# Columns for the sort by target loaded during the sort by source, and four groups folded before the bits are made, in a graph kernel on one core

## The reference, cut to what matters

```python
for l in range(3):                       # first network
    xi, xj = x[src], x[dst]
    e = relu((xj - xi) @ theta[l].T + xi @ phi[l].T)
    agg = segment_max(e, src)            # by source
    x = relu(batch_norm(agg) * gamma[l] + beta[l])
# second, third and fourth network: sums over edges by target (dst),
# with edge_type (16 kinds) and edge_weight for each edge
```

## Time and profile before

| | |
|---|---|
| median of 3 runs | 7136.56 us (7126.43 to 7139.59) |
| the profiled execution's own time | 7128.72 us |
| its span in the trace | 7127.0 us |
| DVE busy | 4064.9 us (57%) |
| POOL busy | 3651.3 us (51%) |
| PE busy | 2465.0 us (35%) |
| mean granted TensorE clock | 0.664 |

### The profile page before, as it was taken

How to read it: one execution, slowest core, us unless ns; L and a number is a source line. 1 busy time by engine, 2 the same in 40 slices (tenths; PEclk the granted TensorE clock), 3 DMA queues, 4 the chain that set the end, 5 groups by cost and what they waited for, 6 DMA issues and landing times. The chain is left out here.

```text
span 7127.0 us, 70146 instructions
## 1 busy us (share of the span) xinstructions
PE 2465.0 (35%) x10688; PEld 1392.0 (20%) x10714; DVE 4064.9 (57%) x10627; ACT 1532.5 (22%) x3929; POOL 3651.3 (51%) x3557
## 2 busy tenths in 40 slices
PE   4477000445566666980006950011001300000038
PEld 3333000322243333440003420001000300000025
DVE  8997454477757765443335444354445466666661
ACT  1165000122236652113332113320001000000011
POOL 0000577477657760017761037755774477777720
PEclk9999555755587887995558975555555755555569
DMA  0001455466545541336653336643663465655610
GB/s 3 0 0 41 156 192 197 133 204 206 187 135 188 187 166 48 153 122 205 210 196 110 153 136 209 210 140 134 208 207 110 149 190 188 190 185 187 190 63 18
DMA packets 334787, 1052.51 MB, mean 148 GB/s; under 512 B 72272, under 2 KB 107632, under 8 KB 288080
## 3 DMA queue, kind: packets, MB, share of 16 engines
q0 software_dynamic: 181456, 515.80, 24.7%
q1 hardware_dynamic: 153216, 535.47, 19.3%
HBM read 534.80 MB, written 516.19 MB: 147 GB/s over the span
## 5 line engine op out<-in xcount | busy, mean ns | idle before, releaser
L940 POOL DMA_INDIRECT rows<-typed_table,index x832 | 813.0, 977 | 1185.6 <-DVE index L964 932.8
L940 POOL DMA_INDIRECT out_of<-table,index x936 | 970.5, 1037 | 465.1 <-issue 283.9
L979 DVE SCALAR_TENSOR_TENSOR state<-state,by_target_keep,rows 128x256 f32<-128x256 f32 x1248 | 604.9, 485 | 950.1 <-ACT rows L958 544.7
L940 POOL DMA_INDIRECT rows<-table,index x728 | 730.5, 1003 | 317.9 <-issue 221.5
L2211 PE MATMUL bank<-weights,out_of 128*128 128x512 f32 x1600 | 698.8, 595 | 26.6 <-DVE weights L2259 26.6
L979 DVE SCALAR_TENSOR_TENSOR y<-y,by_source_anew,out_of 128x256 f32<-128x256 f32 x897 | 435.9, 486 | 294.9 <-DMA out_of<-table,index 196.6
L1109 PE MATMUL bank<-ident,tail 128*128 128x128 f32 x6 | 2.0, 433 | 1658.2 <-PEq L74 1658.2
L2355 POOL DMA_INDIRECT qv<-qv_table,index x416 | 495.3, 1191 | 143.7 <-issue 126.4
L958 ACT ACTIVATE rows<-rows,by_target_weight 128x256 f32<-128x256 f32 x832 | 343.1, 494 | 753.8 <-DMA rows<-typed_table,index 753.8
L2358 POOL DMA_INDIRECT k<-k_table,index x416 | 433.2, 1041 | 126.8 <-issue 126.8
L1739 PE MATMUL bank<-x,marks 128*128 128x416 f16 x1664 | 395.4, 410 | 218.0 <-ACT marks L1753 218.0
(11 more groups left out here) (438 smaller groups left out, 6513.9 us busy)
## 6 DMA issues: line engine op xcount, KB each, us to landing
states<-state SPq DMA_DIRECT2D x195, 1024.0 KB, 4.3
states<-y SPq DMA_DIRECT2D x117, 1024.0 KB, 4.5
typed_table<-staged SPq DMA_DIRECT2D x400, 256.0 KB, 2.0
wide_states<-y SPq DMA_DIRECT2D x26, 1088.0 KB, 5.6
wide_states<-state SPq DMA_DIRECT2D x26, 1088.0 KB, 5.6
out_of<-table,index POOLq DMA_INDIRECT x936, 2.9
rows<-typed_table,index POOLq DMA_INDIRECT x832, 2.9
rows<-table,index POOLq DMA_INDIRECT x728, 2.9
```

Source lines behind the costliest of these rows:

```text
L940: pool.indirect_dma_start(out=rows[h][:, u * D:(u + 1) * D], out_offset=None, in_=table, in_offset=bass.IndirectOffsetOnAxis(ap=index[h][: ...
L979: nc.vector.scalar_tensor_tensor(out=state[h][:, u * D:(u + 1) * D], in0=before, scalar=marks[:, bass.ds(g * GROUP + u, 1)], in1=rows[h][: ...
```

## The change

The four columns for the sort by target are loaded by SP during the first step of `edge_order`, after POOL has filled their tiles; the edge type goes straight to `by_target.row`, and the source shifted by 4 is put in by an OR. `TargetSort.pad` fills only `z`. In the first pass DVE waits for the remaining four loads, folds groups 0 to 3, then runs `CountTargets.ahead`, and then the one-hot tiles of the groups 0 to 3 in one run; from group 4 on each group's one-hot tiles follow its fold as before. The second and third pass are as they were.

```diff
--- before.py
+++ after.py
@@ edge_order
-def edge_order(nc, env, order):
+def edge_order(nc, env, order, target, given):
...
-        names = ("hot", "w_ready", "turned", "copied", "counted", "count_kept", "compared", "ranked", "held")
+        names = ("hot", "w_ready", "turned", "copied", "counted", "count_kept", "compared", "ranked", "held", "padded", "loaded")
...
+            columns = ((target.node, given["dst"], ROWS - 1), (target.source, given["src"], ROWS - 1), (target.row, given["edge_type_16"], 0),
+                       (target.weight, given["edge_weight"], 0.0))
+
+            @block.gpsimd
+            def _(pool):
+                for tile, _, fill in columns:
+                    pool.memset(tile[:], fill).then_inc(padded, 1)
+
+            @block.sync
+            def _(sp):
+                sp.wait_ge(padded, len(columns))
+                for tile, dram, _ in columns:
+                    sp.dma_start(tile[0:P - 1, :], dram[0:(P - 1) * STEPS].rearrange("(p t) -> p t", t=STEPS)).then_inc(loaded, 16)
+                    sp.dma_start(tile[P - 1:P, 0:TAIL], dram[(P - 1) * STEPS:E].unsqueeze(0)).then_inc(loaded, 16)
+                sp.wait_ge(loaded, 32 * len(columns))
+
@@ edge_pass
-                def fold_group(i, h, more=True):
+                def fold_group(i, h, more=True, alone=False):
...
-                    if beside:
+                    if beside and not alone:
                         beside.group(dve, g, h % 2)
...
-                if beside:
+                late = bool(beside) and beside.late
+                if beside and not late:
                     dve.wait_ge(loaded, 16 * len(loads))
                     beside.ahead(dve)
                 for h in range(RING):
-                    fold_group(0, h)
+                    fold_group(0, h, alone=late)
+                if late:
+                    beside.ahead(dve)
+                    for h in range(RING):
+                        beside.group(dve, h, h % 2)
@@ TargetSort (CountTargets.late = True, PlaceTargets.late = MoveTargets.late = False)
-        self.kind = lent.take(STEPS, I32)
-        self.given = given
-        self.columns = [(order.node, given["dst"]), (order.source, given["src"]), (self.kind, given["edge_type_16"]), (order.weight, given["edge_weight"])]
-
-    def loads(self):
-        for tile, dram in self.columns:
-            yield tile[0:P - 1, :], dram[0:(P - 1) * STEPS].rearrange("(p t) -> p t", t=STEPS)
-            yield tile[P - 1:P, 0:TAIL], dram[(P - 1) * STEPS:E].unsqueeze(0)
...
-        nc, order = self.nc, self.order
-        for tile, fill in ((order.node, ROWS - 1), (order.source, ROWS - 1), (self.kind, 0), (order.weight, 0.0)):
-            nc.vector.memset(tile[:], fill).then_inc(done, 1)
-        nc.vector.memset(self.z, 0.0).then_inc(done, 1)
+        self.nc.vector.memset(self.z, 0.0).then_inc(done, 1)
@@ CountTargets.ahead
-        then(nc.vector.tensor_single_scalar(order.row[:], order.source[:], 4, op=ALU.logical_shift_left))
-        then(nc.vector.tensor_tensor(out=order.row[:], in0=order.row[:], in1=sort.kind, op=ALU.bitwise_or))
+        then(nc.vector.tensor_single_scalar(part[:], order.source[:], 4, op=ALU.logical_shift_left))
+        then(nc.vector.tensor_tensor(out=order.row[:], in0=order.row[:], in1=part[:], op=ALU.bitwise_or))
@@ relative_block
-            if layer == 0:
-                loads += sort.loads()
```

More of the change, by code:

```diff
@@ L222, in tile_of @@
             return buffer[:, bass.ds(g * (GROUP * width) + u * width, width)]
-        names = ("hot", "w_ready", "turned", "copied", "counted", "count_kept", "compared", "ranked", "held")
-        with phase(nc, *names) as (hot, w_ready, turned, copied, counted, count_kept, compared, ranked, held), \
+        names = ("hot", "w_ready", "turned", "copied", "counted", "count_kept", "compared", "ranked", "held", "padded", "loaded")
+        with phase(nc, *names) as (hot, w_ready, turned, copied, counted, count_kept, compared, ranked, held, padded, loaded), \
                 nc.Block() as block:
+            columns = ((target.node, given["dst"], ROWS - 1), (target.source, given["src"], ROWS - 1), (target.row, given["edge_type_16"], 0),
[11 more added lines that the diff above has]
+                sp.wait_ge(loaded, 32 * len(columns))
             turn_bank = [env.bank[h][:].bitcast(BF16) for h in range(2)]
@@ L1411, in __init__ @@
         self.z, self.col_a, self.col_b = lent.take(STEPS * BITS, BF16), lent.take(STEPS), lent.take(STEPS)
-        self.kind = lent.take(STEPS, I32)
-        self.given = given
-        self.columns = [(order.node, given["dst"]), (order.source, given["src"]), (self.kind, given["edge_type_16"]), (order.weight, given["edge_weight"])]
-    def loads(self):
-        for tile, dram in self.columns:
-            yield tile[0:P - 1, :], dram[0:(P - 1) * STEPS].rearrange("(p t) -> p t", t=STEPS)
-            yield tile[P - 1:P, 0:TAIL], dram[(P - 1) * STEPS:E].unsqueeze(0)
     def pad(self, done):
-        nc, order = self.nc, self.order
-        for tile, fill in ((order.node, ROWS - 1), (order.source, ROWS - 1), (self.kind, 0), (order.weight, 0.0)):
-            nc.vector.memset(tile[:], fill).then_inc(done, 1)
-        nc.vector.memset(self.z, 0.0).then_inc(done, 1)
+        self.nc.vector.memset(self.z, 0.0).then_inc(done, 1)
 class CountTargets:
+    late = True
     names = ("bits_made", "hot", "turned", "copied", "tallied", "summed", "totalled", "held")
@@ L1515 @@
 class PlaceTargets:
+    late = False
     names = ("masked", "hot_tile", "alike", "compared", "code_met", "hot_block", "crossed", "hot_row", "tallied", "running", "added",
@@ L2879, in graph_program @@
             edge_columns(nc, env, given["src"], given["dst"])
-            edge_order(nc, env, by_source)
+            edge_order(nc, env, by_source, by_target, given)
         by_source.end_row = by_target.end_row = buffer(stack, nc, "end_row", ROWS, BF16)
```

## The result

The changed kernel takes 7072.19 us (median of four runs, 7067.61 to 7075.56). The kernel before, with a fourth run beside it, takes 7131.5 (7120.81 to 7139.59). The profiled execution took 7067.61 us with a span of 7065.9, 61.1 less than before, at the same mean TensorE clock (0.665 against 0.664).

The account below looks back on a forecast made before the run. POOL's gather pace was taken to bound the first pass, after a 40.57 us gap before its 33rd gather. The 65th gather 39.1 us earlier, other terms 0, gave 7089.6 or 7097.5, middle 7094; range 7080 to 7112.

Parts of the forecast that it names:

- the sum of the two sides: First pass, 65th gather: the later of DVE's 794.2 and POOL's 794.8, 39.1 us earlier; no further difference counted behind it.
- The forecast of 39: Whole kernel: gain of 39 us, all from the 65th gather of the first pass coming earlier.
- First gather: Start of first pass: four fills leave first_rows, gain 2.2 us (1.7 to 2.4), first gather at 708.0.
- 33rd gather: First pass with loads moved out: POOL ready 40.6 us after the first gather, at 748.6, no stall left.
- Bits: DVE behind fold 3: bits from 754.5 to 783.3, 25.4 us alone plus 3.4 lost beside 18 gathers.
- One-hot runs: DVE after the bits: four groups' one-hot tiles take 5.7 us to 789.0, PE keeping up; then fold 4 takes 4.2.
- POOL's side: Gathers of groups 4 to 7: 43.3 us plus 2.9 beside the bits, 46.2 in all, so 65th gather at 794.8.
- its upper bound: POOL beside the bits: twelve 1.04 us operations each hold a gather throughout, 12.5 us for 2.9, 65th gather at 804.4.
- The loads: Sort by source: fills and loads, about 45 us, hidden in a 243 us step that DVE ends; cost taken as 0.
- Rival A: First pass: gathers stand still while the bits are made; gain 17.5 us, time about 7115; chance 0.06.
- B: Loads not hidden, or the wait only moves (late weights, PE holding one-hot tiles); 7119 or more; chance 0.03.
- C: Later PE stages, line 2211: TensorE's clock rises later, 100 matmuls at the lower level give 7154; chance 0.02.

Follow-up runs that it names:

- either part alone: Against the kernel before: only the loads moved, order of the pass as it was, 7099.8 us (0.9963); only the order of the pass changed, loads left, 7100.3 us (0.9975).

## Why the prediction was wrong

The sign and the mechanism aimed at were right; the size was not, and it failed at one step.

**The step that failed** is the sentence on DVE behind the sum of the two sides: it "catches up in the same way, so I count no further difference". I took POOL's pace after the 65th gather as the same in both kernels. It was 10.78 us for a group before and 10.13 after, 28.1 us over the rest of the pass; in its place the runs showed gathers held by `hot_b`, at a price of 30 us in the kernel before (7130.0 to 7100.2 without it). The profile before had the sign of it: the second pass, with other companions and the same gathers, went at 10.23. I read the earlier trace rows as an undisturbed POOL, because it never waited, and the loss was in the duration of its instructions. The counts of gathers for 100 us would have shown a loss of 5 to 6%, and the runs' spread of 13 us would have been a question to ask.

How the 59 us split: with `hot_b` in pieces in both kernels, where a group takes 10.18 and 10.21 us and so the pace hardly differs, the change is worth 7100.2 - 7071.4 = 28.8 us by the medians, 34.0 at the 65th gather, 32.6 at the last, and 36.5 by the spans of the two profiled executions (7107.7 and 7071.2). The stalls are thus worth about 29 to 37. The forecast of 39 for them lies a little above all of these. The rest is the rhythm, which the kernel before has nearly throughout in its trace and the changed one hardly. All of the rhythm would be worth 30 (the pieces' gain in the kernel before). That the time fell below the range and not inside it is therefore partly luck of the run: at 47 us of gain it would have been about 7084.

**The steps by themselves:**

1. First gather at 708.0 forecast, 706.92 measured. The right time by another sum: the gap of 0.64 us stayed, so the fills gave 1.75 us, and the table's last copies, in front of the fills, came 1.5 us earlier. That second part varies: in the five other undisturbed traces without the fills the first gather comes at 707.65 to 708.46.
2. 33rd gather at 748.6 forecast, 747.62 measured, with 0.30 us idle before it. Right.
3. Bits: start 754.5 forecast, 754.42 measured; length 28.8 forecast, 25.5 measured (754.42 to 779.96). My 3.4 us for DVE, carried over from the earlier trace rows, did not occur: 1.03 and 0.38 us as if alone.
4. One-hot runs: 5.7 us forecast, 5.66 measured; PE did not hold them up. Fold 4: 4.2 forecast, 4.73 measured (785.65 to 790.38), as in the kernel before for a fold of the loop behind the first four groups (807.79 to 812.52). The index copy came at 790.38, 2.9 earlier than forecast since the bits were shorter, and POOL didn't wait for it.
5. POOL's side decided, as forecast, but for groups 4 to 7 it took 49.05 us (747.62 to 796.67), not 46.2. The gathers that met one of the twelve 1.04 us bit operations took 1.59 to 1.64 us, one in each bit's 1.90 us: 12 x 0.65 = 7.8 us above an undisturbed 40.0. Of the other 1.2, 1.0 went beside the four one-hot runs (1.46 us for one gather, 1.11 for three) and the rest beside folds: the collision with `hot_b` stood already here. The forecast had counted 2.9 us beside the bits, the third pass's price for shorter operations, and 12.5 for the twelve at its upper bound; 7.8 lies in the middle of the two. The 65th gather came at 796.67, forecast 794.8.
6. The loads: hidden. Right. The price of a column is not where one would look: SP's records give 0.22 to 1.18 us for the 127 rows and 2.73 to 8.25 for the one-row piece behind them, in each of the four columns. Whether that piece is slow itself or waits for the rows ahead of it, no run shows.

Rival A (gathers stand still) did not occur: 14 gathers went out while the bits were made (18 forecast), twelve of them longer by 0.65 us. Nor did B: no wait took the place of the stalls. Nor C: line 2211, now 2221, has 592/592/1192 ns for its 1600 matmuls. The forecast's range took in the unknown price of the collision with the bits, which lasts 25 us, but not the same kind of collision with `hot_b`, which comes with each of the 44 groups behind.

**What stays open** is what puts a run into one rhythm. Once DVE has caught up with the gathers, the change as a whole goes on in the fast one in both its undisturbed traces, and so does the one with the one-hot operations exchanged; either part alone, and a stall put back, are slow at that point. But these are one or two traces of each kernel, and four of them change over in the middle of the pass, so that chance has a part in it. Nothing that I ran separates the two.

## To carry to other kernels

A queue that never waits is not one that runs undisturbed: count its instructions in windows of 100 us, and compare the mean duration of one with the shortest. Where two engines follow each other group by group, an edit somewhere else can shift the phase in which they meet, for the rest of the loop; a forecast needs a term for it, and its range the size of that term (here 30 us). Here it paid to cut the operation that held the other engine into pieces, even though the pieces take longer together (1.42 us for 1.2).

## What the runs showed of the hardware

- A gather that begins inside the two-input `hot_b` takes what is left of it and 0.81 to 0.83 us: 1.11, 1.17, 1.49, 1.85 and 1.94 us in five cases (0.95 undisturbed), the first of them with 0.29 us left. One that began 0.11 us before `hot_b` lost nothing. DVE's own operation was 1.21 or 1.22 us in either case.
- The one-input bit operations with a stride in their output (1.03 us) hold a gather in another way: it begins 0.44 us before one of them, at 756.47 for 756.91, and ends 0.12 us behind it, at 758.06 for 757.94.
- Beside four pieces of 0.42 us the gather took 1.10 us; it began inside the last of them, by the same rule (0.28 us left and 0.82).
- Beside the bits, whose three operations repeat every 1.90 us, the gathers fall into step with them: one in each 1.90 us, where 1.25 is their own pace.
